# Experts of a decoder layer: ten shared blocks ahead of the routed tiles and six behind, in place of twelve and four

## The chip, the cores and the metric

The kernel runs on one core of a Trainium2 chip. The metric is the device time of one execution in microseconds (us). A core has five engines that run their own instruction streams and meet at semaphores: TensorE (PE, matrix products; PEld is its loading of weights), VectorE (DVE), ScalarE (ACT), GpSimd (POOL) and SyncE (SP, which here issues DMAs). Sixteen DMA engines move data between the device's main memory and the on-chip memory SBUF. Products land in PSUM.

## The reference, cut to what matters

The kernel computes one decoder layer on 4 sequences of 1024 tokens with 256 channels: three self-attentions, a cross-attention, and a mixture of experts, each followed by an addition and a layer norm. The change touches the experts alone. There, 8 routed experts and one shared expert each have a gate, an up and a down matrix (256 x 512, 256 x 512, 512 x 256), and each token uses its two best routed experts and the shared one:

```
scores = softmax(x @ gate_w)
topk_w, topk_idx = top_k(scores, 2);  topk_w = topk_w / (sum(topk_w) + 1e-20)
for e in range(8):
    hid = silu(x @ w_gate[e]) * (x @ w_up[e])
    y = y + w_per_expert[:, e:e+1] * (hid @ w_down[e])
shared = silu(x @ ws_gate) * (x @ ws_up) @ ws_down
x = layernorm(x + y + shared)
```

## The kernel before, in words

All of it happens in `run_experts`. The 4096 tokens are cut in two ways.

**Shared blocks.** The shared expert takes the tokens in order, 256 at a time: 16 blocks (`SHARED`), numbered 0 to 15 here. A block is two halves of the hidden width. For each half TensorE makes the gate and the up product (`shared_hidden`, product line 50), each in three terms because a number is held as a rounded upper part and a residual. ScalarE applies silu (line 2728), VectorE multiplies (`product`, line 2936), rounds the result to the upper part (the cast, line 2941) and takes the residual (line 2943). TensorE then makes the down product (`shared_down`, line 2598), and VectorE adds it to the tokens' row (`accumulate`, line 2959).

**Routed tiles.** Each token is sent twice, once to each of its experts. The 8192 rows are sorted by expert into 71 tiles (`NTILE`) of 128 rows. GpSimd fetches a tile's rows from main memory with an indirect DMA (`fetch`, line 2502), ten tiles ahead (`NX`). TensorE turns them over (`turn`, line 2625), ScalarE and VectorE split them (lines 2744 and 2953), TensorE makes the gate and up products, turns the hidden values (line 2632) and makes the down product (line 2657). ScalarE scales it by the expert's share (`keep`, line 2750), and GpSimd writes it back to the token's place (line 2537).

**The order.** It is written out by hand. `SH1` blocks come ahead of the tiles (12), the other `SH2` (4) behind them. Beside the first eight blocks VectorE works out the routing in steps (`PICK1` to `SPLIT`, then `mark` and, with block 8, `index`, line 2931), so the first row fetch can be issued after block 8. The row fetches are issued back to back: ten of them. The tiles begin when block `SH1 - 1` is done (`turn(0, 0, 0)`, then `turn(1, 1, 0)`), and SyncE then loads the second expert's matrices into the place where the shared expert's lay (`load(1, 0)`, behind `wait_ge(y_ready, BT * SH1)`); the shared expert's matrices come back in the last load, before the closing blocks. On TensorE the blocks ahead are unrolled, and the closing blocks are one unrolled block and a loop over the others. On VectorE and ScalarE both are unrolled.

**The joining.** When the last tile is written back, GpSimd signals `all_back`. SyncE fetches the two routed results of 256 tokens (a pair of row tiles, `fetch(q)`, line 2484), three pairs ahead (`NGB`). GpSimd sums the two results (line 2548), VectorE adds the sum to the tokens' rows (`combine`, line 2967) and takes mean and variance (lines 2970 and 2976), ScalarE takes the root (line 2759), VectorE makes reciprocal and shift (`slopes`, lines 2980 and 2983), ScalarE normalises (line 2765), and SyncE stores the pair (line 2495). A fetch further ahead waits in SyncE's queue behind the store of an earlier pair. There are 16 such pairs. In each closing block but the first, two of them are joined (`PER`): `joined(c)` names them, their `combine` stands behind the block's second residual on VectorE, their root and `normalise` stand in the next block on ScalarE (whose table of functions is changed for the root and back for silu). The `JOINED` pairs are so done beside blocks, and the rest follow the last block: the tail.

```
FIRST = 2 * SH1
SECOND = FIRST + NTILE
JOINED = PER * (SH2 - 1)
def joined(c):
    return range(PER * (c - 1), PER * c) if c > 0 else ()
```

The results of the first eight blocks go to a side buffer (`early`, `ASIDE`), because their rows are still being written to main memory for the routing; from block 8 on they are added in place.

Of the kernel before, what the change touches and what calls it, by code (L numbers as in the profile page):

```python
# [391 lines left out]
SHARED = TOK // (BT * P)  # L392
# [1948 lines left out]


ASIDE = SHARED // 2
SH1 = 3 * SHARED // 4


NX = 10
# [2 lines left out]
def run_experts(nc, A, scr, ident, xa, xb, acc, w, out):  # L2350
# [4 lines left out]
    with ExitStack() as stack:  # L2355
        k = Kit(nc, stack, "ex")
        TT = TOK // P
        SH2 = SHARED - SH1
        BLOCK = BT * P
        WS = 2 * EW  # L2360
        NGB = 3
        FIRST = 2 * SH1
        SECOND = FIRST + NTILE
# [93 lines left out]
        def _(sp):  # L2457
            def load(expert, n):
                sp.dma_start(w[:, n], scr["ws"][expert * P:(expert + 1) * P]).then_inc(w_in, 16)
# [11 lines left out]
            sp.wait_ge(routed, 2)  # L2471
            sp.wait_ge(y_ready, BT * SH1)
            load(1, 0)
            sp.wait_ge(w_in, 16)
            sp.sem_inc(w_ready, 1)
            for e in range(2, NE + 1):

                freed = sp.value_load(until[0:1, e - 2:e - 1], min_val=1, max_val=BT * SH1 + NTILE)
                sp.wait_ge(y_ready, freed)
# [73 lines left out]
        def _(pe):  # L2553
# [65 lines left out]
            def turn(i, buf, uses):  # L2619

                pe.wait_ge(rows_in[buf], 16 * uses + 16)
                if not (isinstance(i, int) and i == 0):
                    pe.wait_ge(xb_done, i)
                for kh in range(KH):
                    last = pe.transpose(psx[:, kh, 0:SLOTS], xrow[:, buf, kh * P:(kh + 1) * P], ident[:])  # L2625
                last.then_inc(xT_ps, 1)
# [11 lines left out]
            def expert_of(i):  # L2638
                return pe.value_load(which[0:1, bass.ds(i, 1)], min_val=0, max_val=NE - 1)
# [32 lines left out]
            pe.wait_ge(experts_in, 32)  # L2672
            for c in range(SH1):
                if c == PLACE:
# [10 lines left out]
            turn(1, 1, 0)  # L2685
            pe.wait_ge(acc_done, BT * SH1 + BT)
            e = expert_of(0)
# [458 lines left out]
```

## Time and profile before

| | |
|---|---|
| Median of three runs | 3077.74 us (3074.71 to 3079.04) |
| The profiled execution's own time | 3069.23 us |
| Its span (first to last instruction) | 3067.5 us |
| TensorE's mean granted clock | 0.954 of full speed |
| Experts, from about 2476 us to the end | some 591 us |
| One load of an expert's matrices (line 2459 or 2463) | 3072 KB |

Times in the rows are counted from the span's start. The experts are its last fifth: twelve blocks to 2631.4, tiles to 2985.3, four blocks to 3026.8, the tail to the end. A busy time of TensorE is not TensorE at its peak, since its products are pipelined. "Idle before" in a row is the time the engine stood still before it, with the engine that ended the wait.

### The profile page before, as it was taken

The numbers are of one execution on the slowest core, as the hardware profiler recorded it, in microseconds if no ns is written. First come the engines' busy times: TensorE is split into PE (matmuls) and PEld (weight loads), VectorE is DVE, ScalarE is ACT, GpSimd is POOL, SyncE is SP. The second block draws the span as 40 slices with busy tenths as digits, with TensorE's granted clock in tenths as the row PEclk, the third lists the DMA queues.
The fourth block names the chain that finished last, engine by engine and source line by source line (L and its number), as shares of the span: only waits on it lengthen the run. The fifth ranks groups of instructions, "written<-read, shape, count | busy, mean of one in ns | idle before, by whom it ended". The sixth has DMA issues, their size and how long they took to land. (4 is left out here: it accounts for less than half of the span.)

```text
span 3067.5 us, 42743 instructions
## 1 busy us (share of the span) xinstructions
PE 2766.0 (90%) x14144; PEld 1789.4 (58%) x14145; DVE 2051.0 (67%) x3049; ACT 1414.2 (46%) x2550; POOL 966.6 (32%) x986
## 2 busy tenths in 40 slices
PE   7989999999999799999998999659999578999994
PEld 6754445455555345555554555446666458888883
DVE  4568777777777388878877887446655756333336
ACT  2215666666666544444444445324444323233334
POOL 5467530000000054444435554460100510243422
PEclk9979999999999899999999999869999789999997
DMA  6988985454441255555554542265654432313335
GB/s 224 316 243 273 241 218 72 57 69 61 65 64 27 48 124 153 155 160 160 146 169 123 143 129 87 98 140 102 108 98 78 130 138 65 117 53 135 140 117 167
DMA packets 245934, 399.99 MB, mean 130 GB/s; under 512 B 37584, under 2 KB 147768, under 8 KB 244472
## 3 DMA queue, kind: packets, MB, share of 16 engines
q1 hardware_dynamic: 177684, 251.20, 31.1%
q10 hardware_dynamic: 49299, 82.70, 12.7%
q0 software_dynamic: 18768, 63.79, 6.6%
q8 instruction: 99, 1.62, 0.2%
q14 instruction: 84, 0.68, 0.1%
HBM read 231.46 MB, written 166.14 MB: 130 GB/s over the span
## 5 line engine op out<-in xcount | busy, mean ns | idle before, releaser
L655 DVE TENSOR_REDUCE an_m<-an_psm 128x1 f32<-128x1024 f32 x512 | 604.4, 1220 | 162.9 <-PE an_psm L579 162.2
L635 ACT ACTIVATE an_probs<-an_pst 128x512 f32<-128x512 f32 x1024 | 533.9, 603 | 307.3 <-PE an_pst L606 305.8
L1408 ACT ACTIVATE wj_probs<-wj_pst 128x512 f32<-128x512 f32 x512 | 298.1, 596 | 349.9 <-PE wj_pst L1250 340.7
L1125 POOL TENSOR_TENSOR wj_sums<-wj_sums,wj_probs 128x512 f32<-128x512 f32 x192 | 267.1, 1391 | 315.0 <-ACT wj_probs L1408 311.7
L1439 DVE TENSOR_REDUCE wj_m<-wj_pm 128x1 f32<-128x512 f32 x512 | 324.1, 680 | 18.2 <-PE wj_pm L1225 17.8
L579 PE MATMUL an_psm<-an_ks,an_qs 127*128 127x512 f32 x768 | 262.8, 423 | 4.3 <-DVE an_m L655 4.3
L606 PE MATMUL an_pst<-an_qs,an_ks 128*128 128x512 f32 x768 | 251.8, 406 | 3.5 <-ACT an_probs L635 3.3
L1239 PE MATMUL wj_pacc<-wj_probs,wj_vs 128*64 128x512 f32 x1024 | 250.0, 609 | 2.8 <-ACT wj_probs L1408 2.8
L579 PEld LDWEIGHTS an_psm<-an_ks,an_qs 127*128 127x128 f32 x768 | 130.1, 189 | 176.0 <-issue 142.8
L591 PE MATMUL an_pacc<-an_probs,an_vs 128*32 128x512 f32 x1536 | 205.2, 606 | 9.1 <-ACT an_probs L635 8.2
L1250 PE MATMUL wj_pst<-wj_qs,wj_ks 128*128 128x512 f32 x512 | 204.0, 398 | 0.0
L1165 POOL MEMSET wj_qs<- 64x2048 f32 x2 | 3.5, 1800 | 613.4 <-issue 613.4
L606 PEld LDWEIGHTS an_pst<-an_qs,an_ks 128*128 128x128 f32 x768 | 143.3, 188 | 89.7 <-ACT an_probs L635 55.0
L1125 DVE TENSOR_TENSOR wj_sums<-wj_sums,wj_probs 128x512 f32<-128x512 f32 x192 | 180.2, 939 | 20.3 <-ACT wj_probs L1408 20.2
L2296 DVE TENSOR_REDUCE ac_mneg<-ac_psm 128x4 f32<-128x616 f32 x128 | 102.5, 801 | 118.0 <-PE ac_psm L2200 118.0
L2936 DVE TENSOR_TENSOR ex_hid<-ex_gated,ex_pu 128x512 f32<-128x512 f32 x103 | 70.8, 688 | 154.2 <-PE ex_pu L50 100.4
L2273 ACT ACTIVATE ac_probs<-ac_pst 128x1024 f32<-128x1024 f32 x64 | 65.6, 1024 | 180.9 <-PE ac_pst L2219 180.9
L2728 ACT ACTIVATE ex_gated<-ex_pg 128x512 f32<-128x512 f32 x103 | 61.7, 599 | 178.8 <-PE ex_pg L50 176.3
L1248 PE MATMUL wj_pst<-wj_qs,wj_ks 128*128 128x512 f32 x320 | 132.7, 415 | 10.2 <-ACT wj_probs L1408 10.2
L2537 POOL DMA_INDIRECT scr_ys<-ex_yrow,ex_xrow x71 | 69.3, 976 | 212.1 <-ACT ex_yrow L2750 206.0
L1239 PEld LDWEIGHTS wj_pacc<-wj_probs,wj_vs 128*64 128x64 f32 x1024 | 62.6, 137 | 124.4 <-issue 98.1
L579 PE MATMUL an_psm<-first_k,first_q 127*128 127x512 f32 x256 | 103.2, 496 | 12.6 <-DVEq L679 7.1
(434 smaller groups left out, 5980.9 us busy)
## 6 DMA issues: line engine op xcount, KB each, us to landing
ew_w<-scr_ws SPq DMA_DIRECT2D x10, 3072.0 KB, 14.3
scr_ws<-wide_pair POOLq DMA_DIRECT2D x27, 1024.0 KB, 5.4
an_qs<-scr_q SPq DMA_DIRECT2D x48, 256.0 KB, 11.7
an_ks<-scr_k SPq DMA_DIRECT2D x48, 256.0 KB, 13.4
ac_qs<-scr_xq ACTq DMA_DIRECT2D x48, 256.0 KB, 5.5
wj_qs<-scr_mq ACTq DMA_DIRECT2D x18, 512.0 KB, 5.0
wj_ks<-scr_mk ACTq DMA_DIRECT2D x18, 512.0 KB, 6.0
scr_xs<-x_acc SPq DMA_DIRECT2D x2, 4128.0 KB, 16.1
```

The source lines that it names most:

```text
L579: last = pe.matmul(psm[:, n % 2, kh], qs[slot][0:MROW, j, q0:q0 + P], ks[slot][0:MROW, j, kh * CH:(kh + 1) * CH], start=True, stop=True)
L591: last = pe.matmul(pacc[j * AH:(j + 1) * AH], vs[slot][:, kc, j * AH:(j + 1) * AH], probs[:, s % 2, j], start=(kc == 0), stop=(kc == KC - 1))
L606: pe.matmul(pst[:, n % RING], ks[g][:, j, kc * P:(kc + 1) * P], qs[g][:, j, qh * CH:(qh + 1) * CH], start=True, stop=True).then_inc(st_rea ...
L635: act.activation(probs[:, s % 2, j], pst[:, (GH * s + j) % RING], ACT.Exp, scale=HD ** -0.5).then_inc(exp_done, 1)
L655: dve.tensor_reduce(m1[:, hq, col:col + 1], psm[:, n % 2], AX.XY, ALU.max).then_inc(mx_done, 1)
L1125: eng.tensor_tensor(sums[:, x % CPB, j], earlier, probs[:, s % RING, j], ALU.add).then_inc(sum_done[j], 1)
L1239: last = pe.matmul(pacc[j * BHD:(j + 1) * BHD], vs[:, slot, kc, j * BHD:(j + 1) * BHD], probs[:, s % RING, j], start=(kc == 0), stop=(kc = ...
L1248: pe.matmul(pst[:, j], ks0[G % SLOT][:, j, kc * P:(kc + 1) * P], qs0[G % SLOT][:, j, qh * CH:(qh + 1) * CH], start=True, stop=False)
L1250: pe.matmul(pst[:, j], ks1[:, G % 2, j, kc * P:(kc + 1) * P], qs1[:, G % 2, j, qh * CH:(qh + 1) * CH], start=False, stop=True).then_inc(st ...
L1408: act.activation(probs[:, x % RING, j], pst[:, j], ACT.Exp, scale=BHD ** -0.5).then_inc(exp_done, 1)
L1439: dve.tensor_reduce(m1[:, hq, kh, col:col + 1], pm[:, part % MB], AX.X, ALU.max).then_inc(mx_done, 1)
L2296: dve.tensor_reduce(mneg[:, hq, 0:GH * NT].rearrange("p (j i) -> p j i", i=NT)[:, :, i], scores, AX.XY, ALU.max, negate=True).then_inc(mx_ ...
```

## The change

One constant is changed, the number of shared blocks ahead of the routed tiles:

```diff
 ASIDE = SHARED // 2
-SH1 = 3 * SHARED // 4
+SH1 = 5 * SHARED // 8
```

With `SHARED` = 16, `SH1` goes from 12 to 10, so `SH2` goes from 4 to 6 and `JOINED` from 6 to 10. `FIRST`, `SECOND`, the semaphore values and the loops over blocks follow from it. `index` stays at block 8, and the side buffer stays at eight blocks. Blocks 10 and 11 are now made behind the tiles.

## Rows read from the trace of the kernel before

**Rows 1.** the page: each engine's busy time in us

```profile
PE 2766.0 (90%) x14144; PEld 1789.4 (58%) x14145; DVE 2051.0 (67%) x3049; ACT 1414.2 (46%) x2550; POOL 966.6 (32%) x986
```

**Rows 2.** windows of the experts: TensorE, its loads, VectorE, ScalarE, GpSimd, clock, DMA

```profile
2476.00:2606.70 130.70, 112.92 (x868) 101.00 (x869) 77.12 (x158) 33.81 (x102) 8.10 (x28) 0.95 0.36 118
2606.70:2631.40 24.70, 20.47 (x147) 20.07 (x145) 8.83 (x17) 2.39 (x4) 4.35 (x5) 0.86 0.11 32
2631.40:2985.30 353.90, 348.91 (x2121) 306.82 (x2120) 127.87 (x214) 130.87 (x282) 127.57 (x130) 1.00 0.34 120
2985.30:3026.80 41.50, 37.32 (x300) 36.12 (x299) 28.25 (x65) 15.10 (x26) 10.43 (x8) 1.00 0.29 96
3026.80:3067.50 40.70, 0.22 (x2) 0.02 (x1) 26.53 (x97) 17.76 (x39) 12.68 (x10) 0.56 0.69 220
```

**Rows 3.** the chain over blocks 9, 10 and 11: start, length, what

```profile
2597.24 1.44 PE ex_pg L50 x12
...
2606.74 1.44 PE ex_pg L50 x12
2608.18 1.44 PE ex_pu L50 x12
2609.62 1.44 PE ex_pg L50 x12
...
2616.27 5.46 PE ex_py L2598 x24
...
2629.74 1.70 PE ex_py L2598 x12
```

**Rows 4.** timeline of ScalarE and of VectorE in block 10

```profile
2611.27 0.60 ACT L2728 ACTIVATE ex_gated<-ex_pg 128x512 f32<-128x512 f32 x1 [9.07 <-PE ex_pg L50]
...
2614.25 0.69 DVE L2936 TENSOR_TENSOR ex_hid<-ex_gated,ex_pu 128x512 f32<-128x512 f32 x1 [6.86 <-PE ex_pu L50]
```

**Rows 5.** GpSimd's first and tenth row fetch; GB/s in half us from 2598

```profile
2599.79 1.12 POOL L2502 DMA_INDIRECT ex_xrow<-scr_xs,ex_rows_of  x1 [67.69 <-DVE ex_rows_of L2931]
...
2611.32 0.95 POOL L2502 DMA_INDIRECT ex_xrow<-scr_xs,ex_rows_of  x1 [0.30 <-issue]
...
GB/s 0 0 0 0 0 0 0 157 107 41 182 41 149 116 41 206 17 140 124 41 190 33 140 124 25 215 25 132 132 41 198 25 0 0 0 0 0 0 33 0
```

**Rows 6.** the expert matrices' load, on SyncE's queue

```profile
2631.52 0.33 SPq L2459 DMA_DIRECT2D ew_w<-scr_ws  x1
```

**Rows 7.** ScalarE, first and last step before the first tile's second half

```profile
2631.69 0.38 ACT L2744 ACTIVATE ex_xsa<-ex_psx 128x256 fp32r<-128x256 f32 x1 [4.80 <-PE ex_psx L2625]
...
2638.53 0.60 ACT L2755 ACTIVATE ex_ha<-ex_psh 128x512 fp32r<-128x512 f32 x1 [0.90 <-PE ex_psh L2632]
```

**Rows 8.** the chain, the starts of blocks 13, 14 and 15

```profile
2996.22 1.44 PE ex_pg L50 x12
...
3007.01 1.44 PE ex_pg L50 x12
...
3016.49 1.44 PE ex_pg L50 x12
```

**Rows 9.** timeline of VectorE's casts in blocks 14 and 15, and of GpSimd

```profile
3013.59 0.43 DVE L2941 CAST ex_ha<-ex_hid 128x512 fp32r<-128x512 f32 x1
...
3023.08 1.48 DVE L2941 CAST ex_ha<-ex_hid 128x512 fp32r<-128x512 f32 x1
...
3022.99 1.28 POOL L2548 TENSOR_TENSOR ex_got<-ex_got 128x512 f32<-128x512 f32 x1 [0.47 <-DMA ex_got<-scr_ys]
```

**Rows 10.** SyncE's fetch of pair 7 and GpSimd's sum of it

```profile
3028.22 0.47 SPq L2484 DMA_DIRECT2D ex_got<-scr_ys  x1
...
3033.61 1.27 POOL L2548 TENSOR_TENSOR ex_got<-ex_got 128x512 f32<-128x512 f32 x1 [0.72 <-DMA ex_got<-scr_ys]
```

**Rows 11.** one tile's view, the gathered rows: the joining adds of 16 pairs

```profile
L2967 DVE TENSOR_TENSOR x_acc<-ex_early,ex_got x8: 672/686/694, 3005.2 to 3035.0; 128x512 f32<-128x512 f32 x8
L2967 DVE TENSOR_TENSOR x_acc<-x_acc,ex_got x8: 693/694/694, 3037.9 to 3060.0; 128x512 f32<-128x512 f32 x8
```
## The prediction

> **What bounds the kernel now.** I read the page's busy times first, then windows over the experts, then the chain of waits, then single engines' timelines around the two places that the edit touches. TensorE is busy for 90% of the span [rows 1], so a reordering can only gain where TensorE is not the limit. The windows [rows 2] show where that is. Up to 2985.3 TensorE is nearly full (348.91 of 353.90 us in the routed tiles). The closing shared blocks take 41.5 us with 37.32 busy. Then come 40.7 us with TensorE at 0.22: the tail, in which the pairs of rows that no block has covered are fetched, summed, normalised and stored. Those are ten pairs now. A second loss lies just ahead of the routed tiles: blocks 10 and 11 take 24.7 us, of which TensorE is busy for 20.47 [rows 2].
>
> The chain [rows 3] splits these two. Block 9 runs from 2597.24 to 2606.74, 9.5 us. Block 10 runs to 2621.73, 15.0 us. Block 11 ends at 2629.74 + 1.70 = 2631.44, 9.7 us. Block 10 is therefore 5.3 us too long. Its cause shows in the timelines [rows 3, 4]: the gate product ends at 2609.62 - 1.44 = 2608.18, yet ScalarE starts on it at 2611.27, 3.1 us later; the up product ends at 2609.62, yet VectorE starts at 2614.25, 4.6 us later. TensorE's signals, or the work behind them, came late. At that time GpSimd writes the ten row fetches, from 2599.79 to 2612.3, and their bytes move until 2614.0 [rows 5]. The lateness ends when they end. That they cause it is likely but not shown: at one each 1.28 us six of them were already issued in block 9, which lost nothing [rows 3, 5]. Part of the 5.3 is the clock: the 24 down products take 5.46 us where two dozens at 1.70 take 3.4, and the mean granted clock of the stretch is 0.86, so below the upper of its two levels (2.4 GHz) for a part of it, after TensorE had waited [rows 2, 3].
>
> **The change part by part.** One constant falls from 12 to 10. Every loop, wait value and unit number is derived from it, so the same products, fetches, loads, sums and stores are issued. They move in four ways.
>
> (a) The tail. The pairs joined beside blocks are two for each closing block but the first: 2 x 5 = 10, not 6. Four pairs leave the tail. The joining add of the eighth pair starts at 3035.0 and that of the sixteenth at 3060.0 [rows 11], so one pair costs 25.0 / 8 = 3.13 us, and four cost 12.5. From below, VectorE's 26.53 busy us over ten pairs [rows 2] make 2.65 each, 10.6 for four; from above the whole tail over ten pairs makes 4.07 each, 16.3 for four. I take **-12.5**, since the row of the adds is the pace itself, without the tail's start and end, which stay.
>
> (b) Two blocks leave the stretch ahead of the tiles: **-24.7**, block 10's 15.0 and block 11's 9.7 [rows 3].
>
> (c) Two blocks come at the end, each with two pairs beside it. Blocks 13, 14 and 15 start at 2996.22, 3007.01 and 3016.49, and the last ends at 3026.8 [rows 8, 2]: 10.8, 9.5 and 10.3 us, 10.2 on average. Two cost **+20.4**; the ends are 19.0 and 21.6. What two pairs add to a block is 16 small VectorE instructions (an add, two statistics, two aggregates, a reciprocal and two slopes each), six of ScalarE with two table loads, two sums on GpSimd and four DMAs on SyncE. All but the table loads only move out of the tail, and they lie beside the products: block 14 has them all and still takes the 9.5 us of block 9. Without that cover they would cost the 2.65 us of VectorE for each pair that (a) has. What is left over 9.5 us is a collision. The cast in block 14 takes 0.43 us; in block 15 it takes 1.48, beside GpSimd's sum, which runs for 1.28 us from 3022.99 [rows 9]. The cast stands between the hidden product and the down product, so TensorE waits for it.
>
> The Trainium skill (SBUF — State Buffer, "Who interferes with whom") says that VectorE and GpSimd share a pair of ports that the first to start holds for its whole instruction, a cast among the kinds that want it. The cast of 1.48 us agrees. It speaks against this change, which puts four more sums beside blocks: if each held the full 1.28, the sum below would be 4 x 1.28 - 1.4 = 3.7 us worse.
>
> The pairs arrive in time. Pair 7 is fetched at 3028.22 and its sum starts at 3033.61 [rows 10], and ends at 3034.9. In the new order such a fetch would be followed by a block like one that begins at 3026.8. The adds stand behind the block's second cast, which is 6.6 us in (3013.59 against 3007.01 [rows 8, 9]) and is followed by about a microsecond of its own and its residual: 3034.5 for the first pair, and pair 7 is the second. So the fetch is covered, but by a microsecond or so; a wait of VectorE for GpSimd's sum would be what is late next, and with it the next block's hidden product, which is queued behind it.
>
> (d) The routed tiles start 24.7 us nearer to the row fetches. The index is ready as before, so the ten fetches run from 2599.79 and end at 2614.0 [rows 5], but the first tile now starts at 2606.7 rather than at 2631.4. Its own rows are there (the first fetch's bytes move from 2601.5, and the second's and third's before 2606). Yet the lateness that cost block 10 5.3 us now falls on the first tile's start. Also on SyncE the load of the second expert's matrices, 3 MB, moves from 2631.52 [rows 6] to 2606.8, beside what is left of the row fetches on the DMA engines; GpSimd's queue holds nothing after them that is due before the first tile's result. The second expert is wanted only when the first one's tiles are done, so the load itself I cost at nothing. The price of the lateness is from 0 (it belongs to block 10's own code) to 7.3 (2606.7 to 2614.0: nothing passes until the fetches are done). I take **+5.3**, what block 10 shows: the fetches are the only thing in the rows that ends with it, and they do not move.
>
> Nothing else moves: the tokens' rows are written before block 8, eight blocks still add into the side buffer, and the ten joined pairs need blocks 0 to 9, which are all ahead of the tiles.
>
> The sum: -12.5 - 24.7 + 20.4 + 5.3 = -11.5. Against the profiled execution's 3069.23 that is 3057.7; that execution is 8.5 under the median of the three runs, 3077.74, so against the median it is **3066.2**. A measurement of this kernel can tell about 0.2%, 6.2 us, from no change.
>
> **The rivals.**
> No lateness: the 5.3 us belong to block 10 alone, so they go for good. For it: block 9, under the same fetches, lost nothing. Against it: the end of the fetches and of the lateness coincide. -16.8, **3060.9**.
>
> VectorE becomes the bound of the closing blocks. Both GpSimd sums of each block shut out a cast or residual, 1.48 - 0.43 = 1.05 each: a block is 9.5 + 2.1 = 11.6, two are 23.2. For it: VectorE is busy for 28.25 of 41.5 us there [rows 2] and blocks 13 and 15 are long. Against it: block 14 isn't. -8.7, **3069.0**.
>
> All at its worst: that, 7.3 for the start, and 10.6 for the tail: -4.8, **3072.9**, which is no change that can be told.
>
> Slower. The first tile's start is a row of hand-offs with nothing beside them, from ScalarE's 2631.69 to its 2638.53 [rows 7]: five from TensorE to ScalarE (three sets of turned rows, one gate product, one turned hidden). If each is late by the 4.6 us of block 10, where TensorE at least had products to go on with, the start costs 23 instead of 5.3: -16.8 + 23 = +6.2, **3083.9**. It decides from 16.8 / 5 = 3.4 us each. Against it: the fetches end at 2614.0, which leaves room for two such waits, unless the matrices' load keeps it up.
>
> That the constant does not do what it says is ruled out by the derived loops.
>
> **How the numbers follow.** Forecast 45%, no lateness 27%, VectorE the bound 12%, all at its worst 10%, slower 6%. Faster takes the first three, 84%; the same 10%; slower 6%. The bounds of the terms alone give -16.3 - 24.7 + 19.0 = -22.0 (3055.7) and -10.6 - 24.7 + 21.6 + 7.3 = -6.4 (3071.3). The range reaches from 3058, below the no-lateness case, to 3073, the worst without the slower one.
>
> **What would show it.** In the profile after: TensorE idle after the last block for about 28 us, not 40.7, with six joining adds behind it, still about 3.1 apart; closing blocks of 9.5 to 10.8 us; the first tile starting at about 2606.7 and a gap of about 5 us within its first steps that ends near 2614; the load of the second expert at about 2606.8. A tail that loses under 10 us, closing blocks over 11.5, or routed tiles waiting for rows or matrices would prove a step wrong, and a start-up over 13 us longer the forecast as a whole.

## The result and the profile after

| | before | after |
|---|---|---|
| Median, first timing (four runs each) | 3078.39 us (3074.71 to 3087.01) | 3052.11 us (3045.31 to 3057.89) |
| Profiled execution, own time | 3069.23 us | 3057.89 us |
| Span | 3067.5 us | 3056.1 us |
| Experts, from the first load of matrices to the end | 590.6 us | 577.3 us |

The ratio is 0.991, interval 0.9881 to 0.9939: faster, by 26 us in medians. That lies outside the range given, 3058 to 3073, at its fast end. The two profiled spans are 11.4 us apart, which happens to be the forecast's 11.5, but not by its terms. The windows of the changed kernel, cut at the events of [rows 2] (start of the experts, the last blocks ahead, which are now block 9 alone, first tile, closing blocks, tail), show this. The columns are those of [rows 2].

```profile
2478.80:2600.20 121.40, 105.69 (x795) 93.40 (x796) 71.56 (x144) 32.61 (x100) 2.33 (x14) 0.93 0.37 123
2600.20:2609.70 9.50, 8.90 (x75) 8.70 (x73) 5.47 (x14) 1.19 (x2) 5.38 (x6) 1.00 0.22 57
2609.70:2963.40 353.70, 348.70 (x2121) 307.15 (x2120) 127.78 (x214) 130.80 (x283) 131.52 (x135) 1.00 0.35 122
2963.40:3027.60 64.20, 56.57 (x444) 55.03 (x442) 46.20 (x114) 27.88 (x46) 15.48 (x12) 0.97 0.35 111
3027.60:3056.10 28.50, 0.03 (x1) 0.00 (x0) 16.72 (x65) 12.45 (x27) 7.58 (x6) 0.58 0.63 203
```

The tail is 28.5 us in place of 40.7. The closing blocks are 64.2 in place of 41.5, so two more cost 22.7. The tiles take the same 353.7, their start included: there is no lateness, though the ten row fetches still run beside it. From the index's end to the end of the program this profile is 14.4 us shorter (454.4 against 468.8), and the phases ahead of the index took 3.0 us longer.

In all that follows one execution, of the kernel a_join6, stands far apart at 3509.55 us; it is left out of that kernel's ratio and mean.

The start of the matrices' load moved as foreseen, into the run of row fetches. In the timelines of SyncE and GpSimd the load is issued at 2609.83 and the last of ten fetches at 2614.31, as against [rows 5, 6]:

```profile
2609.83 0.33 SPq L2459 DMA_DIRECT2D ew_w<-scr_ws  x1
...
2602.80 1.12 POOL L2502 DMA_INDIRECT ex_xrow<-scr_xs,ex_rows_of  x1 [68.90 <-DVE ex_rows_of L2931]
...
2614.31 0.95 POOL L2502 DMA_INDIRECT ex_xrow<-scr_xs,ex_rows_of  x1 [0.30 <-issue]
```

Two things had to be explained: why the lateness was gone, and why the medians differ by 26.3 us where the profiles differ by 11.4.

### The profile page after: what moved, and what is told of

Read it like the earlier page. It is cut to its first block and busy times, and to the rows that moved or that the text cites. A ratio compares the mean times of both kernels' runs of the same rounds, so it can differ in the third digit from the quotient of the medians.

```text
span 3056.1 us, 42765 instructions
## 1 busy us (share of the span) xinstructions
PE 2766.2 (91%) x14144; PEld 1789.8 (59%) x14145; DVE 2045.4 (67%) x3049; ACT 1418.6 (46%) x2554; POOL 964.8 (32%) x986
## 3 DMA queue, kind: packets, MB, share of 16 engines
q10 hardware_dynamic: 49299, 82.70, 12.7%
## 5 line engine op out<-in xcount | busy, mean ns | idle before, releaser
L1248 PE MATMUL wj_pst<-wj_qs,wj_ks 128*128 128x512 f32 x320 | 133.0, 416 | 11.4 <-ACT wj_probs L1408 11.4
L1239 PEld LDWEIGHTS wj_pacc<-wj_probs,wj_vs 128*64 128x64 f32 x1024 | 62.7, 137 | 124.3 <-issue 98.5
## 6 DMA issues: line engine op xcount, KB each, us to landing
an_qs<-scr_q SPq DMA_DIRECT2D x48, 256.0 KB, 11.5
```

The source lines that it names most:

```text
L1239: last = pe.matmul(pacc[j * BHD:(j + 1) * BHD], vs[:, slot, kc, j * BHD:(j + 1) * BHD], probs[:, s % RING, j], start=(kc == 0), stop=(kc = ...
L1248: pe.matmul(pst[:, j], ks0[G % SLOT][:, j, kc * P:(kc + 1) * P], qs0[G % SLOT][:, j, qh * CH:(qh + 1) * CH], start=True, stop=False)
```

## The experiments

In what follows a stretch is told by events of the profile: "index" is VectorE's last step before the row fetches (line 2931), "first scaled tile" is ScalarE's first `keep` (line 2750). "Closing" runs from the last turned hidden tile to TensorE's last product, the tail from there to the end. A mean time is taken over all times of the kernel named. Each series of timings also holds the kernel before itself, called the comparison kernel here. b2, b3 and b4 are the same program, and are called its copies. Every row of the table is one profile, and a_nosum and b_six were timed only in their profiled execution (3051.13 and 3053.07 us), so only their stretches are used.

| profile | index to first scaled tile | closing | tail | experts |
|---|---|---|---|---|
| before | 45.3 | 42.0 | 40.5 | 590.6 |
| b2 | 45.5 | 41.7 | 41.7 | 590.6 |
| b3 | 45.1 | 41.8 | 40.7 | 589.2 |
| b4 | 41.1 | 41.9 | 40.4 | 586.3 |
| b_latefetch | 47.4 | 41.5 | 40.4 | 590.6 |
| b_spread | 41.1 | 41.6 | 40.5 | 584.9 |
| b_six | 41.1 | 41.8 | 40.1 | 584.9 |
| after | 20.4 | 64.6 | 28.5 | 577.3 |
| a2 | 24.8 | 62.7 | 28.7 | 578.5 |
| a3 | 22.8 | 63.0 | 27.8 | 575.8 |
| a4 | 20.5 | 59.9 | 29.3 | 571.2 |
| a_join6 | 25.8 | 59.9 | 34.4 | 581.3 |
| a_nosum | 24.2 | 58.6 | 26.1 | 571.5 |
| a_spread | 20.5 | 59.8 | 29.0 | 571.3 |
| a_spread2 | 20.4 | 62.6 | 28.4 | 573.6 |
| a_sh9 | 24.2 | 72.9 | 21.7 | 581.1 |

### Both kernels again: b2, a2

No edit. For the kernel before:

> The kernel before, once more, with a second profile. Theory A (the lateness of block 10 is part of every execution of the kernel before): block 10 again takes some 15 us, the lateness in it again ends near the last row fetch's landing, and the span lies near 3067. Theory B (the one profile shown was a lucky one, and the median of 3078 has a longer loss that the profile of 3069 did not have): block 10, or another stretch, loses some 10 us more in this profile. Theory C (executions of one kernel differ by several us in the phases ahead of the experts): the start of the experts moves between the two profiles by several us, and the stretch behind it does not.

and for the changed one:

> The changed kernel, once more. In its first profile the routed tiles start without any lateness (8.0 us from the ready index to the first tile), two more closing blocks cost 22.4 us and the tail is 12.0 shorter, so the experts are 14.3 us shorter. Theory A: the same here within 1 us, time 12 to 17 us under the kernel before in medians. Theory B: the medians differ by some 26 us, and this profile is shorter than the first one by 5 us or more in a stretch behind the index.

b2 has the 590.6 us of experts and block 10's lateness once more, so theory B fell: the first profile was not a lucky one. Its time was 3073.97, and the experts began 4.7 us later than in the first profile. Ten times of it spread from 3061.53 to 3085.32, thirty of the comparison kernel from 3061.87 to 3090.36. The three runs from which I had started, 3074.71 to 3079.04, lay close together by chance.

a2 shows the same from the other side. Its ratio is 0.9936 (0.9911 to 0.9961), yet its profiled execution took 3080.72 us: the experts began only at 2500.5, 21.7 us later than in the other profile of the same kernel, and themselves took 578.5. Laid side by side by product, the two part at several places: they are 4 us apart by 420 us, some 9 by 1340, 12 by 1640, and 21 by 2160, in the cross-attention. None of these phases is touched by the edit. Theory C is what these profiles show.

The first tile's start of a2 was late, by 4.3 us. ScalarE's, VectorE's, TensorE's and SyncE's rows of it:

```profile
2631.67 0.42 DVE L2959 TENSOR_TENSOR x_acc<-x_acc,ex_py 128x256 f32<-128x256 f32 x1 [1.01 <-DMA scr_ck<-in_ab]
2631.71 0.33 SPq L2459 DMA_DIRECT2D ew_w<-scr_ws  x1
...
2633.09 0.38 ACT L2744 ACTIVATE ex_xsa<-ex_psx 128x256 fp32r<-128x256 f32 x1 [7.68 <-remote]
...
2634.08 0.41 PE L2625 MATMUL ex_psx<-all_ident,ex_xrow 128*128 128x128 f32 x2 [3.91 <-issue]
```

TensorE turned the first rows over at 2629.79, and ScalarE took them at 2633.09, 2.9 us after their 0.38. SyncE's load and VectorE's addition both hang on the block's last down product, and both came at 2631.7, so three engines that wait for TensorE were late. That is the pattern of [rows 4], and it was at times there in the new order and at times not.

The 4.3 us are not all lateness: behind it the mean granted clock was 0.72 over 2634.0 to 2640.0, where the undisturbed profile has 1.00 over its whole start. And the lateness did not last until the fetches ended: ScalarE's second step came 0.03 us after TensorE's, at 2634.52, as the last fetch was being issued. In a3 ScalarE's first step and its step behind the first gate product were 1.5 and 1.8 us late, and its second, between them, was not. So single signals came late while fetches were running, not all of them.

### Do the row fetches hold the signals back: b_latefetch

```diff
             pool.wait_ge(indexed, 1)
+            pool.wait_ge(y_ready, BT * 11)
             for i in range(NX):
                 fetch(i)
```

> The kernel before, but GpSimd issues the first ten row fetches only when block 10's down products are done. If the fetches cause the lateness of block 10, block 10 takes 9.5 to 9.7 us in place of 15.0, block 11 may be late in its place (the fetches are then beside it), and the time is from 0 to 5 us under the kernel before. If the lateness belongs to block 10's own code or to chance, block 10 is unchanged at 15 us with no fetch in flight.

Block 10 took 9.5 us, where it had taken 15 in before and b2 (and does so in b3 below). The fetches then ran from 2608.5, through block 11, which was all but undisturbed, into the start of the tiles. That start took 19.7 us in place of 12.7. TensorE turned the first rows over from 2617.84 to 2618.22. The timelines of ScalarE, SyncE and GpSimd:

```profile
2619.99 0.95 POOL L2502 DMA_INDIRECT ex_xrow<-scr_xs,ex_rows_of  x1 [0.30 <-issue]
...
2622.96 0.38 ACT L2745 ACTIVATE ex_xsa<-ex_psx 128x256 fp32r<-128x256 f32 x1 [10.40 <-remote]
2622.96 0.33 SPq L2459 DMA_DIRECT2D ew_w<-scr_ws  x1
```

Both engines go on in the same instant, 3 us after the last of the ten fetches was issued and 4.7 us after TensorE's step. So the lateness moves with the fetches. One profile of this kernel alone would not show that, since block 10 was in time in b4 too, which has no edit; it is the late start, beside fetches that had never been there, that speaks. The time is unchanged (0.9998, 0.998 to 1.0015), and so is the experts' stretch.

### Fetches spread: a_spread, b_spread, and the run cut to six: b_six

```diff
-            for i in range(NX):
+            for i in range(6):
+                if i >= 3:
+                    pool.wait_ge(xT_ps, i - 2)
                 fetch(i)
+            fetched = [6]
...
-                    if i - 1 + NX < NTILE:
-                        fetch(i - 1 + NX)
+                    while fetched[0] < min(NTILE, i + NX, 6 + 2 * i):
+                        fetch(fetched[0])
+                        fetched[0] += 1
```

Both kernels have the same edit, and a_spread2 is a_spread with a second profile. b_six is b_spread without its `if` and wait, so six fetches go back to back.

> The changed kernel with the first ten row fetches spread: three at once, three more each behind one turned tile, the last four two per tile behind the first tiles' write-back. Theory F (a run of back-to-back row fetches on GpSimd's queue holds back TensorE's signals after some 7 us, which cost 5.3 us in block 10 before, 4.3 and 5.3 at the first tile's start in two of three profiles of the new order): from the ready index to the first scaled tile there are 20.6 us, as in the one undisturbed profile, never 25; time 0 to 4 us under the changed kernel. Rival (the lateness is chance or the matrices' load): 24 to 26 us again in this profile; no change of time.

> The kernel before with the same spread fetches; only three are issued ahead of the tiles. Theory F: block 10 takes 9.5 us and the first tile's start 12.7 us, so the experts are 5.3 us shorter than 590.6, some 585.3. Rival: block 10 is late even with three fetches, or the first tile's start is late instead, 590 us.

> The kernel before with six row fetches back to back and the other four behind the first tiles. The fetches then end some 8 us after the index is ready, near the end of block 9. Theory F with a delay (signals are held only when the run of fetches is longer than about 7 us): block 10 takes 9.5 to 10 us. If any run of fetches does it at block 10: 15 us again.

> The changed kernel with spread fetches, second profile. Theory F: 20.5 us from the index to the first scaled tile again, experts 571 to 576 us depending on how GpSimd's sums fall against VectorE's casts; time 2 to 7 us under the changed kernel in means, which ten times of each can hardly tell from none.

In a_spread and a_spread2 the first scaled tile comes 20.5 and 20.4 us after the index. In b_spread and b_six block 10 takes 9.5 us and the experts take 584.9 both times. The first tile's start is then 14.3 and not 12.7 as I expected. The same 14.3 stands in b4, an unchanged kernel before that had no lateness either, where a window at the tiles' start shows TensorE fully busy at a mean granted clock of 0.61, so mostly at its lower level (1.2 GHz):

```profile
2632.00:2636.40 4.40, 4.40 (x14) 3.23 (x12) 0.02 (x1) 0.60 (x1) 0.00 (x0) 0.61 0.98 424
```

b_spread and b_six have 0.61 and 0.62 over the same 4.4 us. At 0.61 of full speed 4.4 us hold 2.7 us of work, so this clock costs some 1.7 us by estimate, which is the 1.6. Where block 10 was late, the clock fell right there, after TensorE had waited [rows 2, 3], and was back before the tiles. So the lateness was worth 4.2 us to the whole, not 5.3 (45.3 against 41.1).

Of eleven profiles with ten fetches in a row, eight were late (before, b2, b3, b_latefetch, a2, a3, a_join6, a_nosum) and three not (b4, after, a4). Of the four with a run of six or fewer whose rows were there in time, none was. If the eight late ones had fallen anywhere among the fifteen, they would have missed all four in 1 case of 39. With b_latefetch beside this I take it that a long run of row fetches holds back signals of TensorE in most executions, not in all. That is likely, from few profiles, and not proved. By which path it does so is open: the records show the wait, not the cause. b_six does not show that a run of six is harmless as such, since its fetches had ended before block 10 began.

In times the spread fetches earned nothing that can be seen: 24 times of a_spread and a_spread2 have a mean of 3057.0, standard error 1.5, against 3054.3 for the changed kernel. b_spread has a mean of 3066.6 over ten, against 3068.7 for the copies of the kernel before. The stretch says 3.2 us (572.5 against 575.7), from two profiles and four.

### Blocks moved without their pairs: a_join6

```diff
-        JOINED = PER * (SH2 - 1)
+        JOINED = PER * 3
...
-            return range(PER * (c - 1), PER * c) if c > 0 else ()
+            return range(PER * (c - 1), PER * c) if 0 < c <= 3 else ()
```

> The changed order of blocks (ten ahead, six behind) but with only the six pairs of before joined, so ten pairs stay in the tail. It separates the two halves of the edit. By my terms: -24.7 + 19.0 to 19.4 for two closing blocks without pairs, no tail gain: 5.5 us under the kernel before, TensorE idle for some 40 us at the end. If the joining is what matters (rival: the blocks are only moved) it is within 1 us of the kernel before. If the closing blocks' extra length of 11.2 us comes from the pairs, blocks 14 and 15 of this kernel are back at 9.5 us.

The ratio was 0.9948 (0.9922 to 0.9974), the mean of nine times 3062.5, and the experts took 581.3, or 576 without the 5.3 of lateness in this profile: 9 us off the 585 of the kernel before without its own. So both readings that I had set against each other were off. The tail of ten pairs is 34.4 us, not 40.5. The window of the tail, in the columns of [rows 2], and the first joining adds on VectorE show where the 6 us went:

```profile
3033.60:3068.00 34.40, 0.27 (x3) 0.07 (x1) 21.56 (x82) 12.88 (x30) 8.88 (x7) 0.54 0.58 184
...
3034.25 0.69 DVE L2967 TENSOR_TENSOR x_acc<-ex_early,ex_got 128x512 f32<-128x512 f32 x1
3035.85 0.68 DVE L2967 TENSOR_TENSOR x_acc<-ex_early,ex_got 128x512 f32<-128x512 f32 x1
3037.76 0.69 DVE L2967 TENSOR_TENSOR x_acc<-x_acc,ex_got 128x512 f32<-128x512 f32 x1
3040.00 0.69 DVE L2967 TENSOR_TENSOR x_acc<-x_acc,ex_got 128x512 f32<-128x512 f32 x1
```

The first four are 1.6 to 2.2 us apart, where a steady pair costs 3.1. GpSimd makes seven sums in this tail, ten in that of the kernel before [rows 2]: under the two blocks without pairs SyncE had stored the earlier pairs and fetched three ahead, and GpSimd had summed those. Half of what I had booked as the worth of joining is thus had by two more blocks alone. The joining itself takes the tail from 34.4 to 28.6 (mean of four) and lengthens the closing blocks from 59.9 to 62.6 (mean of four), so it is worth some 3.1 us, not 12.5. With one profile of this kernel that is rough: against the single profiles of the changed kernel it comes to between 1.2 and 5.1. Its last two blocks, without pairs, take 9.5 us each.

### GpSimd's sum left out: a_nosum

```diff
-                pool.tensor_tensor(got[:, q % NGB, :, 0], got[:, q % NGB, :, 0], got[:, q % NGB, :, 1], ALU.add).then_inc(summed, 1)
+                pool.sem_inc(summed, 1)
```

> The changed kernel without GpSimd's sum of the two routed results (the second routed result of each token is left out of the output). Theory P (closing blocks of over 9.5 us are GpSimd's sum shutting VectorE out of a cast or a residual): every closing block with pairs takes 9.5 us, so the closing stretch is 57 to 59 us in place of 62.7 to 64.6. Rival (VectorE's own work, or ScalarE's table loads, make the length): the blocks stay at 10.4 us. The tail gets shorter too, since a pair's sum of 1.3 us stands in its row: some 25 us in place of 28.6.

In the changed kernel's first profile block 11, the first with pairs, is the longest, 11.7 us. VectorE's cast and residual in it, and GpSimd's three sums:

```profile
2980.85 0.96 DVE L2941 CAST ex_ha<-ex_hid 128x512 fp32r<-128x512 f32 x1
2981.85 1.63 DVE L2943 TENSOR_TENSOR ex_hb<-ex_hid,ex_ha 128x512 fp32r<-128x512 f32 x1
...
2978.64 4.30 POOL L2548 TENSOR_TENSOR ex_got<-ex_got 128x512 f32<-128x512 f32 x3 [7.30 <-DMA ex_got<-scr_ys]
```

0.96 and 1.63 stand where 0.43 and 0.69 do beside no sum. In the chain of waits of a_nosum, the first gate products of blocks 11, 12 and 15:

```profile
2975.84 1.44 PE ex_pg L50 x12
...
2985.33 1.44 PE ex_pg L50 x12
...
3013.80 1.44 PE ex_pg L50 x12
```

Each block takes 9.49 us (the four from 2975.84 to 3013.80 take 37.96), with all of VectorE's own work for two pairs and ScalarE's table loads in it. Everything over 9.5 in the closing blocks is GpSimd's sum in VectorE's way. It comes to 62.6 - 58.6 = 4.0 us over ten sums, 0.4 each: most fall beside instructions that they do not disturb. It differs from profile to profile, and the lengths of the casts and residuals follow it. Against a_nosum they are together 4.4, 4.4, 4.8 and 1.7 us longer in after, a2, a3 and a4, and the closing stretch is 6.0, 4.1, 4.4 and 1.3 longer. So it is the longer instructions, and not waits of VectorE for the sum, that make most of it. The rule cited in the prediction (the Trainium skill, SBUF — State Buffer, "Who interferes with whom") agrees with the kinds of instruction that suffer, the cast and the residual, which has both its inputs in SBUF. Its full price of 1.28 us for each sum was not met.

### One block further: a_sh9

```diff
-SH1 = 5 * SHARED // 8
+SH1 = 9
```

with the spread fetches of a_spread.

> Nine blocks ahead, seven behind, twelve pairs joined, with the spread fetches. One step further on the same way: -9.5 ahead, but the first tile now waits for its own rows (the first fetch lands 3.7 us after the index is ready, the block ahead ends 1.5 us before it), some +5; one more closing block with pairs +10.4; two pairs fewer in the tail -6. Sum 0: the same as the changed kernel with spread fetches within 2 us. If the tail shrinks only by 3 us for two pairs (as the half with ten pairs in the tail suggests), it is 3 us slower.

It is some 9 us slower than a_spread: experts 581.1 against 571.3, mean of ten times 3066.4 against 3057.9. The tail did shrink by 7 us. The closing stretch grew by 13.1 (10.3 against a_spread2), where I had 10.4. The larger loss is at the tiles' start, by a wait that I had priced at 5 and that is 10.4:

```profile
2602.41 0.33 SPq L2459 DMA_DIRECT2D ew_w<-scr_ws  x1
...
2604.87 1.12 POOL L2502 DMA_INDIRECT ex_xrow<-scr_xs,ex_rows_of  x1 [67.33 <-DVE ex_rows_of L2935]
...
2612.72 0.66 PE L2629 MATMUL ex_psx<-all_ident,ex_xrow 128*128 128x128 f32 x2 [10.40 <-DMA ex_xrow<-scr_xs,ex_rows_of]
```

The last block ahead now ends before the index is ready, so SyncE issues the 3 MB of matrices before the first row fetch, and the fetch lands with that load, 7.9 us after its issue, where the median of b4's ten is 2.8. No run held the load back, so that the load delays the fetch is likely from this order of events and not shown by itself. After the wait the clock is down as well: a mean of 0.72 over the next 15.3 us, in which the first tile's start is made, where a_spread makes it in 12.4 at 1.00. Ten blocks ahead are the fewest tried that keep the rows' fetch in front of the load.

### Where the other microseconds are: b3, a3, b4, a4

> The kernel before, third profile, for the scatter. The experts take 590.6 us again (they did so twice to 0.1 us), whatever the whole takes; the median of all its times is 3074 to 3077.

> The changed kernel, third profile. Theory S (the edit is worth the 12 to 13.5 us by which the experts' stretch gets shorter, and the rest of the 26 us between the first medians is scatter of the phases ahead of the experts, which has a standard deviation of some 7 us per execution): over ten more times of each the difference of the means is 8 to 18 us and the ratio 0.994 to 0.997. Rival L (the edit makes the phases ahead of the experts faster too, by where the code lies): the difference stays at 18 us or more, and in this profile the experts begin earlier than in that of the kernel before by 5 us or more. The experts take 577 to 579 us.

> The kernel before, as a submitted copy, so that it is timed in the same turn as the changed kernel's copy below. Theory O (a submitted copy of the kernel before runs some 4 to 6 us under the one it is compared with, as 22 times of two copies did: mean 3069 against 3075): mean 3066 to 3071. If there is no such offset: the same mean as the comparison kernel within 3 us.

> The changed kernel, as a copy of the same standing. Theory S with O: mean 11 to 15 us under that of the copy of the kernel before, as the experts' stretch has it (577 against 590). Rival L (the edit also speeds up what lies ahead of the experts): 17 us or more under the copy.

a3 came out at 0.9929 (0.9905 to 0.9952) and a4 at 0.9948 (0.9927 to 0.9968), both against the comparison kernel, while b3, which is the kernel before itself, came out at 0.9983 (0.9966 to 0.9999). Over all timings, 34 times of b2, b3 and b4 have a mean of 3068.7 (standard error 1.2) and 106 of the comparison kernel 3073.8 (0.7), though all are the same program. The gap of 5.1 us is an upper view of it, for it mixes series: within the series of b2, b3 and b4 it is 3.0, 6.5 and 2.2 us, two of the three ratios have an interval that holds 1, and b4 meets what its expectation named as no offset (within 3 us) as well as what it named as one. Against the copies, the 26 times of the changed kernel, mean 3054.3 (1.5), are 14.4 us faster, give or take 3.8. Within the three series that have both, the difference of the means is 13.0, 14.3 and 15.1. The experts' stretch in four profiles of each has means of 589.2 and 575.7, 13.5 apart.

b4 and a4 alone stand at 3067.7 and 3052.6, 15.1 apart: a hair over the 11 to 15 of theory S and under the 17 of rival L. The start of the experts in the profiles gives rival L nothing either: the mean over seven of the old order is 2474.3, over nine of the new 2482.2, so later, if anything. So I take the edit to be worth about 14 us. Where the offset between a copy and the comparison kernel comes from, I did not find. b_latefetch, whose experts took as long as before, had 3074.6 over ten times, 1.7 under the comparison kernel of its series.

## Why the prediction was wrong

The direction was right, and so was where the time is lost and won, with one reason half wrong, in step (a). The predicted time, 3066.2, and the range, 3058 to 3073, missed.

**What failed first** is the step "against the median it is 3066.2", and with it a range that holds only the bounds of the terms. It took the median of three runs, spread over 4.3 us, as the kernel's time. One execution has a standard deviation of 7 us, from phases that the edit does not touch. Three such runs leave the median some 5 us open by estimate, and the new median of four some 4. The same holds for "a measurement of this kernel can tell about 0.2%". The 8.5 us between the profiled execution and the median, which I noted and set aside, was the sign of it. The miss of 3066.2 - 3052.1 = 14.1 us divides so: 9.0 lie between 3077.74 and the copies' mean of 3068.7 (3.9 of them down to the comparison kernel's 3073.8, and 5.1 the gap that stays open), 2.1 are the terms below, 0.8 is what the terms leave of the 14.4 measured, and 2.2 lie between the changed kernel's mean of 3054.3 and the 3052.1 of its first four times. So the stretches were forecast to about 2 us, and the baseline was not. The fast end of the range was also drawn tighter than its own bounds: they gave 3055.7, and it began at 3058. The 3057.7 worked out from the profiled execution stands next to the 3057.89 of the profile after by luck, since single executions of either kernel scatter by some 7.

**Step (d), +5.3 for the lateness** was mis-sized. Its mechanism, a run of row fetches that holds TensorE's signals back, is borne out as far as the profiles go. But it strikes in most executions only: the start was longer by 0, 4.3, 2.4 and 0 us in the four profiles of the changed kernel, 1.7 on average, part of it the lower clock. The rival "no lateness" gave the lateness to block 10's own code; that fell, since it came back at the tiles' start in a2 and in b_latefetch, while two of the four profiles of the changed kernel had none all the same. The rival of five late hand-offs, and with it the slower outcome, never came near: the most that a start lost was 7.0 us, in b_latefetch.

**Step (a), -12.5**, measured 40.8 - 28.6 = 12.2 as a length, but the reason given was half wrong. a_join6 gets 6.4 of it without joining a pair more. The terms add up only because both halves of the edit were made together.

**Step (b), -24.7**: from the index to the first tile 31.2 (mean of four) became 7.9, 23.3. **Step (c), +20.4**: 62.6 - 41.9 = 20.7. The collision of casts and residuals with the sum is shown by a_nosum. The rival that each sum shuts VectorE out by 1.05 us had two blocks at 23.2, and fell too: the collisions come, but not at every sum. The start of the tiles makes up the rest: 14.3 in place of 13.1, so -12.2 - 23.3 + 20.7 + 1.2 = -13.6, against my -11.5. On the copies' mean of 3068.7 that gives 3055.1, and 3054.3 was measured.

## What to carry to other kernels

Before a range is given around a measured median, look at how far single executions of the same program lie apart and in which phase: an edit of 14 us in a kernel whose executions scatter by 7 can only be sized by the stretch that it touches, or by dozens of times against a copy of the same standing. Work that is queued behind other work in a tail can be drained by more cover alone; try the cover without the extra overlap before giving the overlap the credit. And where fetches and a large load end up in the same few microseconds, look at the order in which they are issued: in a_sh9 the next stage waited 10.4 us for rows asked for behind the load.

## What was not expected of the hardware

Ten indirect row fetches issued back to back by GpSimd, 1.25 us apart, go with signals of TensorE to ScalarE, VectorE and SyncE that arrive late in eight of eleven profiles: single hand-offs by 1.4 us (a_nosum) to 6.0 us (b2, where the gate product ends at 2611.8 and ScalarE starts on it at 2617.80), none of them later than about the last fetch's landing. Other hand-offs under the same fetches came in time. In four profiles with six or fewer in a row it was not seen. A row fetch issued 2.5 us behind a 3 MB load landed with it, 7.9 us later, where the median of ten without a load is 2.8. A GpSimd sum beside VectorE's casts and residuals cost the closing blocks 0.4 us on average, and up to 1.1 us where it met one. Copies of one program differed by 2.2 to 6.5 us in their means within a series, which stays unexplained and is little above their scatter.
